# Feed-forward products and expert splits moved into the last cross-attention group's drain

## The chip, the cores and the metric

The kernel runs on one core of a Trainium2 chip. The metric is the time of one execution in device microseconds. Engines: PE (TensorE), ACT (ScalarE), DVE (VectorE), POOL (GpSimd), and SP, which issues most DMAs.

## The reference

A decoder layer in float32 with three residual stages, on x of 16 sequences of 128 tokens and width 256:

```python
x = x + attn(layernorm(x))            # 16 heads of 64, softmax without mask
x = x + xattn(layernorm(x), ctx)      # 16 heads of 16, masked, keys and values from ctx_1024
x = x + ffn(layernorm(x))

def ffn(x):                           # 8 experts, 256 -> 512 -> 256
    logits = x @ gate_w.T + gate_b    # rms-normalised, times rms_w, softmax(logits / 0.5)
    g = top_1(gates); norm_g = g / (g + 1e-6)
    h = gelu(einsum('nd,edh->neh', x, w1) + b1)
    y = einsum('neh,ehd->ned', h, w2) + b2
    return (y * norm_g[:, None, None]).sum(axis=1)
```

Each token goes through all eight experts.

## The kernel before, in words

Tokens are worked in 4 groups of 512 (4 tiles of 128). Three phases follow one another: ph 0 is self-attention, ph 1 cross-attention, ph 2 the feed-forward stage. Operands of products are split into a rounded high part and a low part (`hi` by ACT, `lo` by a DVE subtraction), and a product of two split operands is three matmuls (`three`, L490).

**Slots.** The attention phases are written as slots of a period of 16 (`run`, L311). In each slot every engine goes through its own hand-written order (`PE_ORDER`, `ACT_ORDER`, `DVE_ORDER`, `POOL_ORDER`), in which each step of a quad (scores, exponential, normalising, transposing, copying, product with V) has a lag in slots. At the end of a slot comes what the engine registered as `"slot"`. Behind the last period stands a drain of 20 slots (`DRAIN`), n = 0 to 19, with ph = 2: scores of the last quads in n up to 10, the last transposes in n = 13, the last product with V (quad 15) in n = 15, the second half of the output projection in n = 17 and 18, the residual in n = 18. The slot n = 4 begins near 525 us of the trace, n = 11 near 541.4, n = 15 ends at 551.03.

**Expert weights.** The 32 chunks m (8 experts x 4) of w1 and w2 come through a ring of four staging tiles `wst` (SP, L428). `expert_hi(m)` (ACT, L828) rounds a chunk into `arena`, `expert_lo(m)` (DVE, L880) writes the rest beside it. Four are split in slots 16 to 19 of the drain, behind a wait for the last product with V (`weights`, L830); the others one for each m in group 0 of the expert loop. Groups 1 to 3 find all of them in `arena`.

**The expert loop** (`experts`, L711 on PE, L851 on ACT, L1135 on DVE). PE runs `up(m)` (6 matmuls of 128x512, L490, into bank `H[m % 4]`) and `down(m - 2)` (12 of 128x256, L490, into Y), the gate's logits (L705) behind `up(1)`, and near the end the transposes of the next group's tokens (L651). ACT runs gelu(m) (L856) from `H` into `probs[m % 4]`, then hi(m) (L860) from there into `PT[m % 2]`; DVE runs lo(m) (L880). The waits that matter: `up(m)` for gelu(m-4), since it writes the same bank; hi(m) for `down(m-2)`, since it writes the same half of `PT`; `down(m)` for lo(m). On ACT the order is written out:

```python
for m in range(MCH):
    act.wait_ge(f1_ps, nth(MSTEP, 2, g, m))
    act.wait_ge(h_lo, nth(MSTEP_F4, 2, g, m - 4))
    act.activation(probs[:, m % 4, :], H[m % 4][:, :], ACT.Gelu, ...).then_inc(act_done, 1)
    act.wait_ge(act_done, nth(MSTEP_F4, 2, g, m))
    act.wait_ge(f2_ps, nth(MSTEP_F2, 2, g, m - 2))
    act.activation(PT[:, m % 2, 0, :], probs[:, m % 4, :], ACT.Copy).then_inc(h_hi, 1)
    if isinstance(g, int) and g == 0 and m + LEAD < MCH:
        expert_hi(m + LEAD)
```

`nth(count, ph, g, i)` is the semaphore value at which step i of group g is done; `_F4` and `_F2` add the 4 or 2 credits that POOL gives at the start.

Of the kernel before, what the change touches and what calls it, by code (L numbers as in the profile page):

```python
# [17 lines left out]
GROUPS = 4  # L18
TILES = 4
GT = TILES * P  # L20
QUADS = 16
# [23 lines left out]
def nth(count, ph, g, i):  # L45

    return count.credit + GROUPS * sum(count.per[:ph]) + g * count.per[ph] + i + 1
# [36 lines left out]
def build(nc, x, ctxT, mask, pieces, gateT, biases, rows, out):  # L84
    with ExitStack() as ctx:
# [78 lines left out]

        A0, A1, S0, S1, T, O, Y0, Y1 = (bank(n) for n in ("A0", "A1", "S0", "S1", "T", "O", "Y0", "Y1"))
        S, Y = (S0, S1), (Y0, Y1)
        H = (S0, S1, A0, A1)


        x_in = [sem("x_in0"), sem("x_in")]  # L170
# [94 lines left out]
        def steps(name, ph, g, v, lag=0):  # L265


            v -= lag
            if name == "quad":
                q = v - SCORES[ph]  # L270
                return [(q,)] if 0 <= q < QUADS else []
            if name in ("qk", "v"):
                if ph == 0:
                    j = v - XT_AT - 1
                    return [(j, BOTH)] if 0 <= j < 16 else []
                jobs = (QK1 if name == "qk" else V1)[g > 0]
                return [jobs[v]] if v in jobs else []
            if name in ("qk_out", "v_out", "qk_last", "v_last"):

                own = name.endswith("last")  # L280
                done = [j for j, halves in steps(name.split("_")[0], ph, g, v if own else v - 1)
                        if 1 in halves]
                return [(j,) for j in done if own == (ph == 0 and j == 15)]
            if name == "proj":
                q = v - SCORES[ph]
                if ph == 0:
                    return [(q // 2, (2 * (q % 2), 2 * (q % 2) + 1))] if 0 <= q < QUADS else []
                return {8: [(0, (0, 1))], 9: [(0, (2, 3))], 16: [(1, (0, 1))],
                        17: [(1, (2, 3))]}.get(q, [])
            if name in ("residual", "bias"):  # L290
                at = QUADS - 1 if ph == 0 else RESIDUAL1[g == GROUPS - 1]
                if name == "residual":
                    return [()] if v - SCORES[ph] == at else []
                part = v - SCORES[ph] - at - ((2, 0)[g == GROUPS - 1] if ph == 1 else 1)
                return [(part,)] if 0 <= part < 2 else []
            ahead = ph == 2 or ph == 1 and g > 0
            if name in ("stats", "norm"):
                tiles = (STATS1 if name == "stats" else NORM1)[ahead]
                return [(tiles[v],)] if v in tiles else []
            if name == "aggr":  # L300
                return [()] if v == AGGR1[ahead] else []
            if name in ("xt0", "xt1"):
                k = int(name[2])
                return [()] if v == (XT1[g > 0][k] if ph == 1 else XT_AT + k) else []
            if name in ("xt0_out", "xt1_out"):
                return steps(name[:3], ph, g, v - (ph == 1 and g > 0))
            if name == "ctx":
                return [(g + 1, v - 11)] if ph == 1 and g + 1 < GROUPS and 11 <= v < 15 else []
            raise ValueError(name)
# [13 lines left out]
        def attentions(eng, order, does):  # L323

            run(order, does, 0, 0, ())
            with eng.Fori(1, GROUPS) as g:
                run(order, does, 0, g, ((0, g - 1),))
            run(order, does, 1, 0, ((0, GROUPS - 1),), later=((1, 1),))
            for g in range(1, GROUPS):
                run(order, does, 1, g, ((1, g - 1), (1, g - 2))[:g],  # L330
                    later=((1, g + 1) if g + 1 < GROUPS else (2, 0),))
            run(order, does, 2, 0, ((1, GROUPS - 1), (1, GROUPS - 2)), DRAIN)

        DRAIN = 20
        TURN = 8
        LEAD = 4

        def v2(g, lo, job):

# [146 lines left out]
        def _(pe):  # L486
# [179 lines left out]
            for i in range(2):  # L666
                mm = pe.matmul(Y0[:, 0:D], ones[:, :], b2half[:, i, :], start=i == 0, stop=i == 1)
            mm.then_inc(b2_ps, 1)
            attentions(pe, PE_ORDER, {
                "scores": scores, "transpose": transpose_probs, "pv": probs_v, "proj": project_out,  # L670
                "qk": project_qk, "v": project_v,
                "xt0": lambda ph, g: transpose_group(ph, g, 0),
                "xt1": lambda ph, g: transpose_group(ph, g, 1)})

            def up(g, m):

                pe.wait_ge(act_done, nth(MSTEP_F4, 2, g, m - 4))
# [22 lines left out]
            def logits(g):  # L700
# [7 lines left out]
                                       start=i == 0, stop=i == 3)  # L708
                mm.then_inc(lg_ps, 1)

            def experts(g):  # L711
                last = isinstance(g, int) and g == GROUPS - 1
                for m in range(MCH + 2):
                    if m == MCH - 1 and not last:

                        transpose_tokens(2, g + 1, (T, O), ((lg_v, g * LGV + 1), None))
                    if m < MCH:
                        up(g, m)
                    if m == 1:
                        logits(g)  # L720
                    if m >= 2:
                        down(g, m - 2)

            with pe.Fori(0, GROUPS - 1) as g:
                experts(g)
            experts(GROUPS - 1)

# [2 lines left out]
        def _(act):  # L730
# [97 lines left out]
                act.activation(arena[:, at:at + PIECE], wst[:, m % 4, :], ACT.Copy).then_inc(e_hi, 1)  # L828

            def weights(ph, g, n):  # L830
                if ph == 2 and DRAIN - LEAD <= n < DRAIN:
                    if n == DRAIN - LEAD:

                        act.wait_ge(pv_ps, nth(SLOT_F2, 1, GROUPS - 1, QUADS - 1))
                    expert_hi(n - DRAIN + LEAD)
                if ph == 0 and isinstance(g, int):
                    for i in weight_slots(n):
                        weight_hi(i)
                    if n == 3:
                        act.wait_ge(b2_ps, 1)  # L840
                        act.activation(b2sum[:, :], Y0[:, 0:D], ACT.Copy).then_inc(b2_sum, 1)
                    if n == 15:
                        act.activation(gate[:, :, 0, :], gst[:, :].rearrange("p (k e) -> p k e", k=KD),
                                       ACT.Copy).then_inc(w_hi, 1)
# [33 lines left out]
        def _(dve):  # L878
            def sub_lo(out_, src, hi, sem_):
                dve.tensor_tensor(out_, src, hi.bitcast(F32), ALU.subtract).then_inc(sem_, 1)  # L880
# [142 lines left out]
            def xt_low(ph, g, k):  # L1023
                tokens_lo(ph, g, (A1, A0), (k,))

            def expert_lo(m):
                at = m * 2 * PIECE
                dve.wait_ge(e_hi, m + 1)
                sub_lo(arena[:, at + PIECE:at + 2 * PIECE], wst[:, m % 4, :], arena[:, at:at + PIECE],
                       e_split)  # L1030

            def weights(ph, g, n):
                if ph == 2 and DRAIN - LEAD <= n < DRAIN:
                    expert_lo(n - DRAIN + LEAD)
                if ph == 0 and isinstance(g, int):

                    late = weight_slots(n) if n < 8 else weight_slots(n - 1) if n > 8 else ()
                    for i in late + (weight_slots(n) if n == PERIOD - 1 else ()):
                        weight_lo(i)
                    if g == 0 and n == 12:  # L1040
                        constants()
                    if n == 15:
                        dve.wait_ge(w_hi, N1 + N2 + 1)
                        sub_lo(gate[:, :, 1, :], gst[:, :].rearrange("p (k e) -> p k e", k=KD),
                               gate[:, :, 0, :], w_split)
# [89 lines left out]
            def experts(g):  # L1135
                last = isinstance(g, int) and g == GROUPS - 1
                for m in range(MCH):
                    dve.wait_ge(h_hi, nth(MSTEP, 2, g, m))
                    sub_lo(PT[:, m % 2, 1, :], probs[:, m % 4, :], PT[:, m % 2, 0, :], h_lo)
                    if isinstance(g, int) and g == 0 and m + LEAD < MCH:  # L1140
                        expert_lo(m + LEAD)
                    if 4 <= m <= 11:
                        gating(g, m - 4)
                    if 14 <= m <= 18:
                        gating(g, m - 6)
                    if not last:
                        if 20 <= m < 24:
                            if m == 20:
                                dve.wait_ge(x_ready, nth(GRP, 1, g + 1, 0))
                                dve.sem_inc(dve_gate, 1)  # L1150
                            ln_stats(2, g + 1, m - 20)
                        if m == 24:
                            ln_finish(2, g + 1)
                        if m == 28:
                            ln_apply(2, g + 1, range(TILES))
                if not last:
                    tokens_lo(2, g + 1, (T, O))
                finish(g)
# [184 lines left out]
```

## Time and profile before

| | |
|---|---|
| median of 3 runs | 937.83 us (937.02 to 937.84) |
| profiled execution | 937.62 us |
| its span, first to last instruction | 935.8 us |
| mean granted TensorE clock | 0.986 |
| PE busy | 866.5 us (93%) |
| ACT busy | 630.3 us (67%) |
| DVE busy | 569.1 us (61%) |
| POOL busy | 291.6 us (31%) |
| clock row of the page, tenths, 40 slices of 23.4 us | 9999999999999999799999999999999999999999 |

The busy shares are means over stages with different limits. What a stage is bound by is read from its own stretch of the trace, and what an idle engine waited for stands in brackets behind the instruction that ended the idle time. A matmul's end is modelled, so that two groups of matmuls that follow each other overlap a little. The granted clock is a share of full speed: 1.00 is 2.4 GHz, 0.50 is 1.2 GHz.

### The profile page before, as it was taken

What the parts mean: (1) busy time and instruction counts of PE and PEld (TensorE: products, weight loads), DVE (VectorE), ACT (ScalarE), POOL (GpSimd) and SP (SyncE); (2) the same over time, 40 slices, a digit from 0 to 9 for tenths busy, and PEclk for the clock granted to TensorE, in tenths of its full rate; (3) what the DMA queues carried; (4) which work ended last, traced back from release to release, by engine and by line L of the source; (5) the groups of instructions that cost most, each with busy time, mean ns of one, the idle gap of its engine ahead of it and who ended that gap; (6) DMA issues with size and microseconds to landing.
All of it is one profiled execution on the core that took longest, in us unless ns stands there. A gap on an engine that the chain in (4) does not pass through costs nothing.

```text
span 935.8 us, 18382 instructions
## 1 busy us (share of the span) xinstructions
PE 866.5 (93%) x6274; PEld 782.3 (84%) x6274; DVE 569.1 (61%) x1172; ACT 630.3 (67%) x1764; POOL 291.6 (31%) x342
## 2 busy tenths in 40 slices
PE   4899999999999987899999879999999999999997
PEld 3788888889888876788888769999999999999996
DVE  4798888788878875677878755454223422342223
ACT  3897788788778864798989856765454445444543
POOL 2254454445445566655746540000000000000000
PEclk9999999999999999799999999999999999999999
DMA  6300000000000005665446113320000000000000
GB/s 207 122 31 18 1 1 1 0 0 0 0 0 0 1 1 137 144 160 113 142 86 171 45 35 102 95 87 6 17 0 0 8 15 0 0 14 9 1 1 22
DMA packets 21770, 41.98 MB, mean 45 GB/s; under 512 B 3144, under 2 KB 3152, under 8 KB 21712
## 3 DMA queue, kind: packets, MB, share of 16 engines
q1 hardware_dynamic: 21120, 40.91, 16.0%
q8 instruction: 32, 0.52, 0.3%
q10 hardware_dynamic: 592, 0.34, 0.2%
q14 instruction: 26, 0.21, 0.1%
HBM read 30.75 MB, written 10.49 MB: 44 GB/s over the span
## 4 chain that ended last, share of the span: by engine, by line
PE 64%; DVE 15%; ACT 13%; issue 5%; DMA 2%; POOL 1%; SPq 1%; DVEq 0%; ACTq 0%; POOLq 0%
PE Y L490 23%; PE A L490 20%; PE S L490 12%; ACT probs L803 7%; PE T L585 3%; DVE PT L880 3%; DVE nm L971 2%; DVE arena L940 2%; DVE oraw L990 2%; PE O L490 2%; PE O L602 1%; DVE arena L880 1%; ACT opart L817 1%; ACT PT L811 1%; DVE st L884 1%
## 5 line engine op out<-in xcount | busy, mean ns | idle before, releaser
L880 DVE TENSOR_TENSOR PT<-probs,PT 128x512 fp32r<-128x512 f32 x128 | 89.7, 701 | 230.9 <-ACT PT L860 230.9
L490 PE MATMUL A<-XT,arena 128*128 128x512 f32 x816 | 217.9, 401 | 6.3 <-DVE arena L940 5.3
L803 ACT ACTIVATE probs<-S,nm 128x128 f32<-128x128 f32 x512 | 181.5, 371 | 45.9 <-DVE nm L971 44.2
L490 PEld LDWEIGHTS Y<-arena,PT 128*128 128x128 f32 x1536 | 200.3, 191 | 11.0 <-DVE PT L880 1.1
L490 PE MATMUL Y<-arena,PT 128*128 128x256 f32 x1536 | 204.0, 283 | 0.3
L1194 POOL TENSOR_TENSOR probs<-probs,rinv 128x512 f32<-128x512 f32 x128 | 133.4, 1042 | 208.4 <-DVE rinv L976 208.3
L490 PEld LDWEIGHTS A<-XT,arena 128*128 128x128 f32 x816 | 144.7, 190 | 36.7 <-DVE arena L940 12.3
L860 ACT ACTIVATE PT<-probs 128x512 fp32r<-128x512 f32 x128 | 80.8, 631 | 90.7 <-PE Y L490 90.2
L803 ACT ACTIVATION_READ_ACCUMULATOR probs<-S,nm 128x1 f32 x512 | 107.4, 210 | 0.0
L880 DVE TENSOR_TENSOR PT<-T,PT 128x512 fp32r<-128x512 f32 x128 | 87.5, 684 | 25.0 <-ACT PT L811 22.8
L971 DVE TENSOR_REDUCE nm<-S 128x4 f32<-128x512 f32 x128 | 87.8, 686 | 18.0 <-PE S L490 10.5
L490 PE MATMUL S<-XT,arena 128*128 128x512 f32 x384 | 98.7, 394 | 0.0
L811 ACT ACTIVATE PT<-T 128x512 fp32r<-128x512 f32 x128 | 76.9, 601 | 23.7 <-PE T L585 21.1
L585 PE MATMUL T<-ident,probs 128*128 128x128 f32 x512 | 80.8, 281 | 5.3 <-DVE PT L880 3.4
L490 PEld LDWEIGHTS S<-XT,arena 128*128 128x128 f32 x384 | 68.7, 190 | 11.5
L490 PE MATMUL Y<-arena 128*128 128x256 f32 x480 | 72.0, 287 | 3.6 <-POOL arena L1216 3.6
L856 ACT ACTIVATE probs<-S,bias 128x512 f32<-128x512 f32 x64 | 44.0, 688 | 42.5 <-PE S L490 42.4
L490 PE MATMUL O<-PT,arena 128*32 128x128 f32 x768 | 60.2, 228 | 12.8 <-ACT oraw L822 7.3
L856 ACT ACTIVATE probs<-A,bias 128x512 f32<-128x512 f32 x64 | 44.0, 687 | 41.6 <-PE A L490 41.6
L990 DVE SCALAR_TENSOR_TENSOR oraw<-O,bias,opart 64x256 f32<-64x256 f32 x128 | 61.0, 477 | 16.5 <-ACT opart L817 14.9
L585 PEld LDWEIGHTS T<-ident,probs 128*128 128x128 f32 x512 | 57.3, 143 | 12.6 <-issue 6.7
L490 PEld LDWEIGHTS Y<-arena 128*128 128x128 f32 x480 | 64.3, 194 | 4.1 <-POOL arena L1216 3.9
(106 smaller groups left out, 1300.9 us busy)
## 6 DMA issues: line engine op xcount, KB each, us to landing
wst<-in_pieces SPq DMA_DIRECT2D x52, 256.0 KB, 2.7
stage<-arena SPq DMA_DIRECT2D x32, 256.0 KB, 2.3
arena<-stage SPq DMA_DIRECT2D x48, 128.0 KB, 4.1
arena<-stage SPq DMA_DIRECT2D x24, 256.0 KB, 3.9
xs<-in_x SPq DMA_DIRECT2D x4, 512.0 KB, 5.8
craw<-in_ctxT SPq DMA_DIRECT2D x4, 512.0 KB, 4.6
out<-craw SPq DMA_DIRECT2D x4, 512.0 KB, 2.6
rowc<-in_rows ACTq DMA_DIRECT2D x1, 264.0 KB, 5.5
```

What stands on the lines that cost most here:

```text
L490: mm = pe.matmul(acc, lhs[a], rhs[b], start=first and i == 0, stop=last and i == 2, skip_group_check=shared)
L585: mm = pe.transpose(T[:, u * P:(u + 1) * P], probs[:, n % 4, u * P:(u + 1) * P], ident[:, :])
L602: pe.matmul(O[:, u * P:(u + 1) * P], v4.rearrange("p s c -> p (s c)"), PT[:, n % 2, 0, u * P:(u + 1) * P], start=True, stop=False, skip_gr ...
L803: last = act.activation(probs[:, n % 4, u * P:(u + 1) * P], S[n % 2][:, u * P:(u + 1) * P], ACT.Exp, bias=nm[:, n % 4, u:u + 1], accum_out ...
L811: act.activation(PT[:, n % 2, 0, :], T[:, :], ACT.Copy).then_inc(pt_hi, 1)
L856: act.activation(probs[:, m % 4, :], H[m % 4][:, :], ACT.Gelu, bias=bias[:, B1 + m:B1 + m + 1]).then_inc(act_done, 1)
L860: act.activation(PT[:, m % 2, 0, :], probs[:, m % 4, :], ACT.Copy).then_inc(h_hi, 1)
L880: dve.tensor_tensor(out_, src, hi.bitcast(F32), ALU.subtract).then_inc(sem_, 1)
L940: last = dve.scalar_tensor_tensor(K[rows_, c % 2, 1, :, h, :], bank[rows_, :].rearrange("p (b c) -> p b c", b=TILES), bias[rows_, BK1 + c: ...
L971: dve.tensor_reduce(nm[:, n % 4, :], s3, axis=AX.X, op=ALU.max, negate=True).then_inc(maxed, 1)
L990: last = dve.scalar_tensor_tensor(oraw[h * DH1:(h + 1) * DH1, n % 2, 0:256].rearrange("p (b c) -> p b c", b=2), o4[:, :, h, :], bias[0:DH1 ...
L1194: pool.tensor_tensor(p3, p3, rinv[:, n % 4, :].unsqueeze(2).to_broadcast([P, 4, P]), ALU.mult).then_inc(normed, 1)
```

## The change

Splits of experts 0 to 5 are made in slots 4, 5, 6, 7, 12 and 13 of the drain instead of 0 to 3 in slots 16 to 19; `LEAD` becomes 6, so that the loop splits expert m + 6 in step m. PE computes `up(0)` to `up(3)` at the end of slots 11 to 14 and the logits and `up(4)` at the end of slot 16, ahead of the second half of the output projection; the banks `H` are ordered so that the first two are the ones that are free then. DVE makes lo(0) and lo(1) in slot 17, ahead of the residual. The token transposes of the feed-forward stage are issued one slot earlier on PE, their evacuation stays in its slot. In group 0 PE's loop starts at m = 5 and `down` lags `up` by 6 instead of 2; the transposes for group 1 stand at m = 34 of 38 instead of 31 of 34. DVE applies the layer norm of the next group at m = 26 instead of 28. Groups 1 to 3 are otherwise as before, and ACT's loop is not touched but for `LEAD`.

```diff
-        H = (S0, S1, A0, A1)
+        H = (A0, A1, S0, S1)
...
+            ahead = ph == 2 or ph == 1 and g > 0
...
-                return [()] if v == (XT1[g > 0][k] if ph == 1 else XT_AT + k) else []
+                return [()] if v == (XT_AT + k if ph == 0 else XT1[ahead][k]) else []
             if name in ("xt0_out", "xt1_out"):
-                return steps(name[:3], ph, g, v - (ph == 1 and g > 0))
+                return steps(name[:3], ph, g, v - ahead)
...
-        LEAD = 4
+        FIRST_EXPERTS = (4, 5, 6, 7, 12, 13)
+        LEAD = len(FIRST_EXPERTS)
+        UP_AHEAD = {11: (0,), 12: (1,), 13: (2,), 14: (3,), 16: (4,)}
+        LOW_AHEAD = (0, 1)
...
+            def experts_ahead(ph, g, n):
+                if ph == 2:
+                    if n == 16:
+                        pe.wait_ge(pt_lo, nth(SLOT_F1, 1, GROUPS - 1, QUADS - 1))
+                        logits(0)
+                    for m in UP_AHEAD.get(n, ()):
+                        if m in (2, 3):
+                            pe.wait_ge(exped, nth(SLOT_F2, 1, GROUPS - 1, QUADS - 4 + m))
+                        up(0, m)
+
+            attentions(pe, PE_ORDER, {
+                "slot": experts_ahead,
...
             def experts(g):
+                first = isinstance(g, int) and g == 0
                 last = isinstance(g, int) and g == GROUPS - 1
-                for m in range(MCH + 2):
-                    if m == MCH - 1 and not last:
+                lag = 6 if first else 2
+                for m in range(5 if first else 0, MCH + lag):
+                    if m == (MCH + lag - 4 if first else MCH - 1) and not last:
 
                         transpose_tokens(2, g + 1, (T, O), ((lg_v, g * LGV + 1), None))
                     if m < MCH:
                         up(g, m)
-                    if m == 1:
+                    if m == 1 and not first:
                         logits(g)
-                    if m >= 2:
-                        down(g, m - 2)
-
-            with pe.Fori(0, GROUPS - 1) as g:
+                    if m >= lag:
+                        down(g, m - lag)
+
+            experts(0)
+            with pe.Fori(1, GROUPS - 1) as g:
                 experts(g)
             experts(GROUPS - 1)
...
             def weights(ph, g, n):
-                if ph == 2 and DRAIN - LEAD <= n < DRAIN:
-                    if n == DRAIN - LEAD:
-
-                        act.wait_ge(pv_ps, nth(SLOT_F2, 1, GROUPS - 1, QUADS - 1))
-                    expert_hi(n - DRAIN + LEAD)
+                if ph == 2 and n in FIRST_EXPERTS:
+                    m = FIRST_EXPERTS.index(n)
+                    if m == 0:
+
+                        act.wait_ge(pv_ps, nth(SLOT_F2, 1, GROUPS - 2, QUADS - 1))
+                    if m == 4:
+
+                        act.wait_ge(scores_ps, nth(SLOT, 1, GROUPS - 1, QUADS - 1))
+                    expert_hi(m)
...
             def weights(ph, g, n):
-                if ph == 2 and DRAIN - LEAD <= n < DRAIN:
-                    expert_lo(n - DRAIN + LEAD)
+                if ph == 2 and n in FIRST_EXPERTS:
+                    expert_lo(FIRST_EXPERTS.index(n))
+                if ph == 2 and n == 17:
+                    for m in LOW_AHEAD:
+                        hidden_lo(0, m)
...
-                        if m == 28:
+                        if m == 26:
                             ln_apply(2, g + 1, range(TILES))
```

`hidden_lo(g, m)` is the pair of lines that was written out in DVE's loop before: the wait for hi(m) and the subtraction lo(m).

## Rows read from the trace of the kernel before

**Rows 1.** Busy time by stretches: us, PE, PEld, DVE, ACT, POOL, clock, DMA share, GB/s
```profile
525.50:535.60 10.10, 8.26 (x85) 6.94 (x83) 8.89 (x19) 9.62 (x41) 4.78 (x6) 1.00 0.00 1
...
541.46:551.03 9.57, 6.21 (x75) 5.04 (x73) 3.78 (x7) 4.47 (x13) 2.90 (x3) 1.00 0.01 2
551.03:554.28 3.25, 0.00 (x0) 0.00 (x0) 1.87 (x2) 3.19 (x6) 2.23 (x2) 1.00 0.01 1
554.28:557.50 3.22, 3.21 (x14) 3.12 (x15) 0.74 (x2) 0.96 (x1) 0.00 (x0) 0.50 0.59 162
...
557.02:650.56 93.54, 93.47 (x601) 84.99 (x601) 49.20 (x93) 60.28 (x97) 5.29 (x4) 1.00 0.25 74
650.56:930.00 279.44, 278.80 (x1794) 253.26 (x1792) 88.29 (x187) 136.65 (x205) 5.04 (x5) 1.00 0.02 6
```

**Rows 2.** Timeline (start us, us, what, idle before): the first products of group 1
```profile
650.56 2.91 PE L490 MATMUL S<-XT,arena 128*128 128x512 f32 x12
```

**Rows 3.** Timeline: a step of the expert loop in group 0
```profile
567.51 1.55 PE L490 MATMUL S<-XT,arena 128*128 128x512 f32 x6
...
568.90 1.59 PE L490 MATMUL Y<-arena,PT 128*128 128x256 f32 x12
...
569.10 0.69 ACT L856 ACTIVATE probs<-S,bias 128x512 f32<-128x512 f32 x1 [0.17 <-PE S L490]
...
570.33 1.55 PE L490 MATMUL S<-XT,arena 128*128 128x512 f32 x6
570.59 0.63 ACT L860 ACTIVATE PT<-probs 128x512 fp32r<-128x512 f32 x1 [0.80 <-PE Y L490]
571.13 0.62 ACT L828 ACTIVATE arena<-wst 128x512 fp32r<-128x512 f32 x1
```

**Rows 4.** Waits, 563 to 650: total us, times, longest
```profile
ACT PT L860 <- PE Y L490: 22.0, 28, 0.8
```

**Rows 5.** Timeline: the drain and the projection behind it
```profile
543.21 0.63 PE L585 MATMUL T<-ident,probs 128*128 128x128 f32 x4 [0.79 <-DVE PT L880]
...
543.76 0.68 ACT L822 ACTIVATE oraw<-O,bias 32x512 f32<-32x512 f32 x1
...
544.46 0.60 ACT L811 ACTIVATE PT<-T 128x512 fp32r<-128x512 f32 x1
...
544.58 0.88 PE L490 MATMUL O<-PT,arena 128*32 128x128 f32 x12 [0.75 <-ACT oraw L822]
545.09 0.69 DVE L880 TENSOR_TENSOR PT<-T,PT 128x512 fp32r<-128x512 f32 x1 [1.15 <-ACT PT L811]
...
554.29 2.93 PE L490 MATMUL Y<-arena 128*128 128x256 f32 x12 [3.27 <-POOL arena L1216]
...
557.26 1.29 DVE L1008 TENSOR_TENSOR xs<-Y,xs 128x512 f32<-128x512 f32 x2 [2.48 <-PE Y L490]
...
560.06 1.85 PE L705 MATMUL T<-gate,XT 128*128 128x16 f32 x16
```

**Rows 6.** Timeline of ACT: the gate's exponential at m = 12
```profile
594.32 1.28 ACT L866 ACT_TABLE_LOAD   x1
...
597.16 0.69 ACT L856 ACTIVATE probs<-S,bias 128x512 f32<-128x512 f32 x1
```

**Rows 7.** Timeline of PE: the idle time ahead of three groups of matmuls
```profile
21.31 2.54 PE L490 MATMUL A<-XT,arena 128*128 128x512 f32 x6 [2.26 <-DVE arena L940]
...
348.86 0.33 PE L602 MATMUL O<-PT,arena 128*128 128x128 f32 x1 [2.29 <-DVE PT L880]
...
517.07 0.88 PE L490 MATMUL O<-PT,arena 128*32 128x128 f32 x12 [1.26 <-DVE arena L880]
```

**Rows 8.** Busy time by stretches: behind two of these gaps, and from 373.50
```profile
21.90:25.00 3.10, 3.10 (x11) 2.50 (x9) 1.49 (x4) 1.11 (x3) 0.00 (x0) 0.50 0.58 184
...
348.86:352.00 3.14, 3.14 (x16) 2.85 (x17) 1.13 (x3) 2.52 (x10) 1.37 (x2) 0.60 0.01 3
...
373.50:387.00 13.50, 9.75 (x41) 8.10 (x42) 9.27 (x24) 8.53 (x42) 11.40 (x11) 0.50 0.86 179
```

More of the change, by code:

```diff
@@ L295, in steps @@
                 return [(part,)] if 0 <= part < 2 else []
-            ahead = ph == 2 or ph == 1 and g > 0
             if name in ("stats", "norm"):
@@ L668, in _ @@
             mm.then_inc(b2_ps, 1)
[L669 to L673, printed above, removed]
             def up(g, m):
@@ L709, in logits @@
                 mm.then_inc(lg_ps, 1)
+            def experts_ahead(ph, g, n):
[9 more added lines that the diff above has]
+                "slot": experts_ahead,
+                "scores": scores, "transpose": transpose_probs, "pv": probs_v, "proj": project_out,
+                "qk": project_qk, "v": project_v,
+                "xt0": lambda ph, g: transpose_group(ph, g, 0),
+                "xt1": lambda ph, g: transpose_group(ph, g, 1)})
             def experts(g):
+                first = isinstance(g, int) and g == 0
                 last = isinstance(g, int) and g == GROUPS - 1
-                for m in range(MCH + 2):
-                    if m == MCH - 1 and not last:
+                lag = 6 if first else 2
+                for m in range(5 if first else 0, MCH + lag):
+                    if m == (MCH + lag - 4 if first else MCH - 1) and not last:
                         transpose_tokens(2, g + 1, (T, O), ((lg_v, g * LGV + 1), None))
@@ L1024, in xt_low, with hidden_lo @@
                 tokens_lo(ph, g, (A1, A0), (k,))
+            def hidden_lo(g, m):
+                dve.wait_ge(h_hi, nth(MSTEP, 2, g, m))
+                sub_lo(PT[:, m % 2, 1, :], probs[:, m % 4, :], PT[:, m % 2, 0, :], h_lo)
             def expert_lo(m):
@@ L1137, in experts @@
                 for m in range(MCH):
-                    dve.wait_ge(h_hi, nth(MSTEP, 2, g, m))
-                    sub_lo(PT[:, m % 2, 1, :], probs[:, m % 4, :], PT[:, m % 2, 0, :], h_lo)
+                    if not (isinstance(g, int) and g == 0 and m in LOW_AHEAD):
+                        hidden_lo(g, m)
                     if isinstance(g, int) and g == 0 and m + LEAD < MCH:
```

## The prediction

> **What bounds the kernel now.** I read the busy shares stretch by stretch first. From the first up product of the feed-forward stage (557.02) to the end, TensorE is busy without a gap: 93.47 of 93.54 us in group 0, 278.80 of 279.44 in groups 1 to 3 [rows 1]. Group 0 runs from 557.02 to 650.56, where the first up product of group 1 starts [rows 1, 2]. Ahead of it lies the hole that the change aims at. In the drain of the last cross-attention group (541.46 to 551.03) TensorE has 6.21 us of work in 9.57; then it has none for 3.25 us while ACT and POOL turn the last output into weights for the output projection; then it runs 3.22 us at half clock (0.50) [rows 1]. The third reading is one step of the expert loop in the order of time [rows 3], and the waits of that loop [rows 4]: ScalarE's rounding copy into PT waits for the down product (PE Y) 28 times, 22.0 us in total. It costs nothing now. With it comes the chain that the change alters.
>
> **The order in the code.** ACT runs, for each chunk m, gelu(m), then hi(m) (the copy into PT[m%2]), in group 0 also the rounding of a later expert, then gelu(m+1). hi(m) waits until down(m-2) has read PT[m%2]. up(m) waits for gelu(m-4), because it writes into the same bank H[m%4]. Now PE runs up(m), down(m-2), so the ring down(m-2), hi(m), gelu(m+1), up(m+5) comes back to PE five steps after it left: slack. In group 0 of the changed kernel PE runs up(m), down(m-6). The ring becomes down(m-2), hi(m), gelu(m+1), up(m+5), **down(m-1)**: it advances by a single chunk, with all of its parts in series. PE runs up(6), down(0), and up(7) has to wait for gelu(3), which stands on ACT behind hi(2), which waits for down(0). This repeats for up(7) to up(31): 25 waits.
>
> **Part 1: expert splits in slots 4 to 7.** They add four ACT roundings and four DVE subtractions to a stretch where ACT is busy 9.62 of 10.10 us and DVE 8.89 [rows 1]. One rounding is 0.62 [rows 3]: 4 x 0.62 = 2.5, less the 0.48 that ACT has free = +2.0 us. Bounds: 0 (the slots are late for PE alone) and +2.5. DVE's four are 4 x 0.69 = 2.8 [rows 5] against 1.2 free, so +1.6 at most, beside ACT's and not on top; I take 2.0. The roundings queue ahead of the next slot's copies and exponentials on ACT, and the transposes wait for these. The transposes of the tokens come one slot earlier on PE and their copies stay: nothing. The loads of experts 4 to 7 are released earlier on SP, in a stretch without other transfers (DMA share 0.00 in [rows 1]): nothing. Splits 4 and 5 in slots 12 and 13 fall where ACT has 4.47 of 9.57 busy: nothing. What they free at the end (the old ones were done under POOL's split) is also nothing.
>
> **Part 2: up(0) to up(4) and the logits in the drain.** One up takes 568.90 - 567.51 = 1.39 us, one down 570.33 - 568.90 = 1.43 [rows 3], the logits 1.85 [rows 5]. A quad of the drain has 12 short products (0.88) and 4 transposes (0.63) [rows 5], about 1.25 where one group overlaps the next; its ring of transpose, ACT copy (0.60) and DVE subtraction (0.69) [rows 5] takes some 2.1 with the semaphores. With an up behind each transpose a slot takes 1.25 + 1.39 = 2.65, PE bound. Walked from the transpose at 543.21 (its 4 take 0.4 before the next can start): pv(12) 545.0, pv(13) 547.7, pv(14) 550.4, pv(15), whose slot before has no transpose, 552.6, its end 553.55, against 551.03: +2.5. Bounds: 0 (the ups fit into the idle time of 3.36 us) and 4 x 1.39 = +5.6 (nothing fits). Then the logits run to 555.3; ACT does the last output (0.68 [rows 5]), a table load for gelu (1.28 [rows 6]) and gelu(0) (0.69 [rows 3]), so up(4) starts about 556.4; the projection is next, at 557.8 and at full clock since no long gap is left; up(5) 559.3, up(6) 560.7, down(0) 562.1 (the residual add, 1.29 [rows 5], is done by 560.8), its end 563.7. With part 1: 565.7.
> Before, down(0) started at about 563.3 with ups 0 to 2 done; now it starts at 564.1 with 0 to 6 done. **The front gains** 4 x 1.39 - 0.8 = 4.8 us.
> Edits at nothing: lo(0) and lo(1) now stand ahead of the residual on DVE and wait for hi(1), which ACT has done at about 558.7, so they end about when the projection does (559.3); down(0), which waits for the residual, is covered by up(5) and up(6), 2.8 us. Without that cover it would cost up to 1.4 us. The new order of H only names free banks; the layer norm at m = 26 runs on a DVE that waits most of its time in the loop.
>
> **Part 3: the serial ring.** Behind the end of a down (568.90 + 1.59 = 570.49) come 0.10 until hi starts (570.59), 0.54 to the expert rounding (571.13) and 0.62 for it [rows 3], 0.69 for gelu, of which some 0.1 overlaps the rounding, and 0.14 until PE starts (as from 543.76 + 0.68 to 544.58 in the drain [rows 5]): about 2.0 us. The cycle is 1.45 (up, after a standstill) + 1.59 (down to its end) + 2.0 = 5.05 against 2.82. up(7) starts at 565.7 + 2.0 = 567.7; up(31) 24 cycles later: 24 x 5.05 = 121.2. Once, at m = 12, ACT loads two tables for the exponential of the gate: 597.16 - 594.32 = 2.84 [rows 6]. Before, the slack swallowed this; now it is in the ring: +2.9. Without the last rounding -0.5. up(31) starts at 691.3.
> The ScalarE: Activation LUTs page of the Trainium skill (What ACT_TABLE_LOAD costs) adds a drain of 1.38 us to each load; by it the two would cost 2.8 us more. The rows show the loads back to back at 1.28 and no drain [rows 6], so the sum leaves it out.
> Behind up(31) come down(25) to down(31) without an up between them. down(m) needs hi(m) (0.63) and lo(m) (0.69) after down(m-2), and with one down between, that is nearly hidden: from up(31) to the first up of group 1 I get 13.0 us, the token transposes included: 704.3. Before: 650.56 [rows 2]. **Sum at full clock: +53.8.** The profiled execution took 937.62 us (span 935.8), which lies 0.2 below the median of 937.83; from there 991.5.
>
> **Part 4: the clock.** In that loop TensorE stands still for 2.0 us in each 5.05. Every single gap of that order in the trace was followed by half clock: 2.26 us at 21.31 (0.50 in 21.90 to 25.00), 2.29 at 348.86 (mean 0.60 in the 3.14 us behind it), the 3.25 before 554.28; the 1.26 at 517.07 was not, by the profile page's clock row in the table [rows 1, 7, 8]. It came back while PE worked without a gap, 3.10 us from 21.90 and 3.21 from 554.28 [rows 1, 8]; at half clock the pair up and down is itself some 5.5 us of dense work. So I expect it to **fall and come back in turns**. A half-clock pair costs 2.93 - 1.59 = 1.3 for the down-like product of 12x256 [rows 3, 5] and at most 1.39 for the up (2.54 against 1.55 where part ran at full clock) [rows 3, 7]: about 2.55. Bounds: no pair (0) to all 25 (+64). I take 10 of 25, since the gap is a little shorter than those that lowered the clock and each fall lasts about one pair: +25.5. **991.5 + 25.5 = 1017.**
> The TensorE: Matmul & The Clock Gate page of the Trainium skill (Why this matters for your kernels) warns of idle gaps between bursts only when they are longer than this loop's. By that rule the clock stays full and the first rival below results; the rows of 2.26 and 2.29 speak against it, as these too are shorter than the page's.
>
> **Rivals.**
> 1. The clock stays full: 991.5. For it: the gap of 2.0 is shorter than any single one that lowered it, and between gaps lie 3 us of dense work. Against: it recurs 25 times.
> 2. The clock stays at half for nearly all of the loop: 991.5 + 24 x 2.55 = 1053. For it: from 373.50 to 387.00 it stayed at 0.50 with PE busy 9.75 of 13.50 us [rows 8]. Against: a half-clock pair gives 5.5 us of unbroken work, more than the 3.10 that raised it at 25.
> 3. Faster: the ring doesn't close, since ACT has gelu(m+1) done before down(m-2) ends. Then only the front's gain counts. Price: up(7) at 565.5, 24 x 2.82 to up(31), 13.0 to group 1: 646.2 against 650.56: 933.3. It decides at up(7). Against it: the 28 waits of hi for PE Y [rows 4], and ACT's order of gelu and hi is not touched by the diff.
> 4. The ups in the drain cost what they bring, and the ring stays open: 937.6, within 0.2%, which is about what a measurement of this kernel can tell from no change.
>
> **How the numbers follow.** Forecast (turns) 70%, rival 1 14%, rival 2 8%, a stall from elsewhere in group 0 that ends slower 3%, rival 3 4%, rival 4 1%. Slower 0.95, same 0.01, faster 0.04. Range: low end is rival 1 less the 2.0 of part 1 and 1.5 of reading error in the walk, 988; the high end takes 19 of 25 pairs at half clock, 1040. That leaves out rivals 2, 3 and 4 and little else.
>
> **What would show it.** In the profile after: ACT's copy into PT in group 0 starts 0.1 us behind each PE Y, and now PE's A and S products wait for ACT's gelu, 25 times, about 2.0 us each; PE is busy some 60% in group 0; the clock row shows digits below 9 in the slices from 570 to 700; group 1 begins near 730; groups 1 to 3 keep their 2.82 a step; the last pv ends near 555.5, and the projection starts without the 3.3 us gap. Wrong would be: PE waiting less than 1 us before an up (rival 3), or a wait for another engine in its place.

## The result, and the profile after

The changed kernel takes 1017.99 us (median of 4, 1016.85 to 1020.16) against 937.84 us (937.02 to 938.42): ratio 1.0858, 95% interval 1.0844 to 1.0871. The forecast was 1017. The profiled execution took 1017.41 us with a span of 1015.6, 79.8 us above that of before. The page:

```profile
PE 899.2 (89%) x6274; PEld 806.3 (79%) x6274; DVE 566.0 (56%) x1172; ACT 626.3 (62%) x1764; POOL 290.7 (29%) x342
...
PEclk9999999999999989999999877777999999999999
```

Between 558 and 711 us (the 23rd to the 28th slice) the clock row falls to 8 and 7, which it did nowhere in group 0 before. Now the loop of group 0, the lines of PE and ACT in the timeline (start, us, what, idle before). It is to be laid beside [rows 3], where up, down, up followed each other at 1.39 and 1.43 us:

```profile
562.40 1.63 PE L493 MATMUL S<-XT,arena 128*128 128x512 f32 x6 [0.69 <-DVE arena L901]
563.86 1.60 PE L493 MATMUL Y<-arena,PT 128*128 128x256 f32 x12
565.55 0.63 ACT L881 ACTIVATE PT<-probs 128x512 fp32r<-128x512 f32 x1 [4.84 <-PE Y L493]
566.09 0.61 ACT L845 ACTIVATE arena<-wst 128x512 fp32r<-128x512 f32 x1
...
566.61 0.67 ACT L877 ACTIVATE probs<-S,bias 128x512 f32<-128x512 f32 x1
...
567.33 1.65 PE L493 MATMUL S<-XT,arena 128*128 128x512 f32 x6 [1.87 <-ACT probs L877]
568.82 1.59 PE L493 MATMUL Y<-arena,PT 128*128 128x256 f32 x12
```

Down the column of starts stands the ring: down(0) at 563.86 ends at 565.46; hi(2) at 565.55; the rounding; gelu(3) at 566.61; up(7) at 567.33, after 1.87 us in which PE waited for gelu. Then the next down, and the same again. PE's waits over the whole execution, ended by gelu (L877), and the stretches (us, PE, PEld, DVE, ACT, POOL, clock, DMA share, GB/s):

```profile
PE A L493 <- ACT probs L877: 26.5, 13, 4.8
PE S L493 <- ACT probs L877: 23.8, 13, 1.9
```
```profile
542.56:554.48 11.92, 11.13 (x101) 9.50 (x99) 4.98 (x9) 5.50 (x15) 2.93 (x3) 1.00 0.16 45
567.33:717.03 149.70, 102.31 (x432) 87.22 (x432) 33.73 (x71) 43.75 (x74) 2.02 (x2) 0.77 0.12 35
717.03:730.39 13.36, 12.92 (x98) 12.26 (x99) 6.06 (x12) 6.44 (x11) 0.00 (x0) 1.00 0.00 1
```

Of these 26 waits 25 are those of up(7) to up(31); the other is up(4) in the drain. In the 149.70 us from up(7) to up(31) PE is busy 68%, at a mean clock of 0.77. Group 1 begins at 730.39 instead of 650.56 [rows 2]: +79.83, the whole difference of the spans. The clock inside the loop, four pairs of up and down of the same timeline:

```profile
591.45 1.66 PE L493 MATMUL S<-XT,arena 128*128 128x512 f32 x6 [1.87 <-ACT probs L877]
592.94 1.59 PE L493 MATMUL Y<-arena,PT 128*128 128x256 f32 x12
596.41 2.53 PE L493 MATMUL A<-XT,arena 128*128 128x512 f32 x6 [1.88 <-ACT probs L877]
598.74 2.30 PE L493 MATMUL Y<-arena,PT 128*128 128x256 f32 x12
602.90 2.24 PE L493 MATMUL A<-XT,arena 128*128 128x512 f32 x6 [1.87 <-ACT probs L877]
604.94 2.57 PE L493 MATMUL Y<-arena,PT 128*128 128x256 f32 x12
609.39 1.94 PE L493 MATMUL S<-XT,arena 128*128 128x512 f32 x6 [1.87 <-ACT probs L877]
611.12 2.76 PE L493 MATMUL Y<-arena,PT 128*128 128x256 f32 x12
615.76 1.65 PE L493 MATMUL S<-XT,arena 128*128 128x512 f32 x6 [1.87 <-ACT probs L877]
```

The waits are the same 1.87 us each time; what changes is the length of the products. Of these four pairs one is at full clock (4.96 us from start to start), the other three take 6.49, 6.49 and 6.37. In the whole loop it is 5 of 24.

### The profile page after: what moved, and what is told of

It is laid out like the page before. It is cut to its first block, busy times and chain, and to the rows that moved or that the text cites. A ratio compares the mean times of both kernels' runs of the same rounds, so it can differ in the third digit from the quotient of the medians.

```text
span 1015.6 us, 18344 instructions
## 1 busy us (share of the span) xinstructions
PE 899.2 (89%) x6274; PEld 806.3 (79%) x6274; DVE 566.0 (56%) x1172; ACT 626.3 (62%) x1764; POOL 290.7 (29%) x342
## 4 chain that ended last, share of the span: by engine, by line
PE 62%; ACT 15%; DVE 14%; issue 6%; DMA 2%; SPq 1%; POOL 0%; ACTq 0%; DVEq 0%; POOLq 0%
PE Y L493 22%; PE A L493 19%; PE S L493 12%; ACT probs L820 6%; PE T L588 3%; DVE PT L901 2%; PE O L493 2%; DVE nm L992 2%; DVE arena L961 2%; DVE oraw L1011 2%; ACT arena L845 2%; ACT probs L877 2%; PE O L605 1%; DVE arena L901 1%; ACT opart L834 1%
## 5 line engine op out<-in xcount | busy, mean ns | idle before, releaser
L493 PE MATMUL A<-XT,arena 128*128 128x512 f32 x816 | 225.1, 412 | 32.5 <-ACT probs L877 26.5
L493 PEld LDWEIGHTS Y<-arena,PT 128*128 128x128 f32 x1536 | 218.8, 208 | 13.0 <-DVE PT L901 1.7
L493 PE MATMUL Y<-arena,PT 128*128 128x256 f32 x1536 | 221.1, 299 | 0.6 <-DVE PT L901 0.4
L493 PEld LDWEIGHTS A<-XT,arena 128*128 128x128 f32 x816 | 148.2, 194 | 66.3 <-ACT probs L877 29.1
L493 PE MATMUL S<-XT,arena 128*128 128x512 f32 x384 | 105.2, 411 | 24.5 <-ACT probs L877 23.8
L1217 POOL TENSOR_TENSOR rstd<-ve,mhalf 128x4 f32<-128x4 f32 x12 | 12.2, 1015 | 225.4 <-DVE ve L916 225.4
L493 PE MATMUL A<-arena,XT 128*128 128x256 f32 x384 | 62.6, 299 | 5.3 <-DVE arena L901 3.3
L877 ACT ACTIVATE probs<-S,bias 128x512 f32<-128x512 f32 x64 | 43.7, 682 | 36.2 <-PE S L493 36.2
```

The lines of the kernel that those rows point to most:

```text
L493: mm = pe.matmul(acc, lhs[a], rhs[b], start=first and i == 0, stop=last and i == 2, skip_group_check=shared)
```

## The experiments

Each is compared with the kernel before on the same chip; where an interval is given, it is of the ratio.

**The lag alone.** Theory: the ring down(m-2), hi, gelu, up(m+5), down(m-1) is the loss. Rival: the work put into the drain is.

```diff
-                lag = 6 if first else 2
+                lag = 5 if first else 2
```

> The changed kernel with one number altered: down lags up by 5 instead of 6 in group 0. Theory (serial ring): with 5 the ring down(m-2), hi(m), gelu(m+1), up(m+5) comes back to PE one pair later, so 2.82 us of PE work lie beside ACT's 1.9 us and the waits vanish but for the one at m = 12 (two table loads, 2.9 us, less 0.9 of slack). down(0) at about 561.8, 26 pairs of 2.82, a tail of 11.8, 2 for the table loads: group 1 begins near 647, so about 934 us, below the kernel before. Rival (the loss comes from doing ups, logits and splits in the drain, or from the deeper lead as such): the waits ahead of the ups stay, and the time stays above 1000 us. If only a part of the ring opened, between 950 and 1000 us.

Measured: 936.77 us against 937.32 (ratio 0.9993, 0.9983 to 1.0003), 81 us less than the changed kernel by one digit. The drain keeps all that the change put there. PE's waits in the loop, and the place at m = 12:

```profile
PE A L493 <- ACT probs L877: 2.0, 1, 2.0
```
```profile
594.53 1.59 PE L493 MATMUL Y<-arena,PT 128*128 128x256 f32 x12
598.15 2.34 PE L493 MATMUL A<-XT,arena 128*128 128x512 f32 x6 [2.03 <-ACT probs L877]
600.29 2.48 PE L493 MATMUL Y<-arena,PT 128*128 128x256 f32 x12
```

24 waits are gone; the one at the two table loads is left, with a stretch of half clock behind it that I had not counted (2.34 and 2.48 against 1.55 and 1.59: from 598.15 to the next up at 602.61 it takes 4.46 instead of 2.82, 1.6 us). The time is 2.8 us above the forecast, and 1.9 of that is a slip in its sum: 561.8 + 26 x 2.82 + 11.8 + 2 is 648.9, not 647. Group 1 begins at 650.50, in an execution that was already 1.7 us behind that of the changed kernel ahead of all that the edit touches: the first scores products of the steady stretch that ends at 541 to 543 us ("the first scores" from here on) started at 396.3 and not at 394.6. The rest is inside the scatter (935.28 to 938.42).

**The lag without the drain.** The kernel before with

```diff
-        LEAD = 4
+        LEAD = 6
...
-                for m in range(MCH + 2):
+                lag = 6 if isinstance(g, int) and g == 0 else 2
+                for m in range(MCH + lag):
```

and `down(g, m - lag)`; no up and no logits in the drain.

> The kernel before with the lag of 6 in group 0 alone: all ups stay in the loop, nothing is moved into the drain; the six splits needed ahead stand in slots 14 to 19. Theory (serial ring): up(0) at 557.0, seven ups, the logits and down(0) to 570.2, then 25 waits of 1.9 us and the same clock as in the changed kernel (24 cycles in about 150 us), tail 13.4: about 1022 us, that is before + 84, more than the changed kernel by what its front gains (4 to 5 us). Rival (the drain part is to blame): about 938 us.

Measured: 1024.72 us (one execution). The lag alone costs 87 us, and the rest of the change brings back some 7. About 1 of these comes from the layer norm at m = 26: with the old m = 28 the transposes for group 1 wait 1.03 us for it at 730.69. PE's waits from 541 to 731 read as those of the changed kernel, though nothing but two more splits was put into the drain:

```profile
PE S L490 <- ACT probs L858: 25.4, 12, 4.8
PE A L490 <- ACT probs L858: 24.1, 13, 2.2
```

**The clock alone.** Five matmuls more behind each down of the ring:

```diff
                         down(g, m - lag)
+                        if first and m < MCH - 1:
+                            for _ in range(5):
+                                pe.matmul(O[:, :], identr[:, :], XT[:, 0, 0, :], start=True, stop=True)
```

> The changed kernel with five more matmuls of 128x512 behind each down in the ring, into bank O that nothing reads at that time: 1.07 us of PE work inside the 1.87 us of idle time, with no new wait. It shows the price of the clock alone. Theory (half clock in turns costs 28 us of the 80): granted clock 1.00 throughout, cycle 4.96, about 990 us though PE does 26 us more work. Rival (the clock is a by-product, and the fillers delay the ups or the clock falls all the same): 1018 us or more.

Measured: 994.85 us (one execution): 23 us less with 27 us of matmuls more. The cycle is 4.95 to 5.0 us, but for the one at the table loads:

```profile
570.23 1.64 PE L493 MATMUL S<-XT,arena 128*128 128x512 f32 x6 [0.71 <-ACT probs L880]
571.71 1.59 PE L493 MATMUL Y<-arena,PT 128*128 128x256 f32 x12
573.14 1.31 PE L741 MATMUL O<-XT,identr 128*128 128x512 f32 x5
575.18 1.66 PE L493 MATMUL A<-XT,arena 128*128 128x512 f32 x6 [0.73 <-ACT probs L880]
...
622.88 2.93 PE L493 MATMUL A<-XT,arena 128*128 128x512 f32 x6 [3.69 <-ACT probs L880]
625.61 2.74 PE L493 MATMUL Y<-arena,PT 128*128 128x256 f32 x12
```

So the clock is a cost of its own and not a by-product. Of the 5 us above the 990 expected, 2.4 are the half clock behind the table loads (7.34 us from 622.88 to the next up, instead of 4.98) and 1.4 that behind the logits in the drain, which the last experiment takes up. The rest, 1.4 us, was there ahead of the drain: the first scores came at 396.0 instead of 394.6.

**A shorter ring.** `expert_hi(m + LEAD)` stands between gelu(m) and the wait for down(m-2) instead of behind hi(m); nothing else is changed.

> The changed kernel with ACT's rounding of the next expert moved ahead of the wait for down(m-2), out of the ring. Theory: the wait ahead of each up shrinks from 1.87 to 1.33 us (by the 0.54 from hi to the rounding), the cycle at full clock from 4.96 to 4.42: 24 x 0.54 = 13 us less from the ring, about 1005 us if the clock falls as often as before; if the gap of 1.33 no longer lowers it (1.26 did not, 2.26 did), about 977 us. Rival (ACT's order is not what the ups wait for): 1018 us.

Measured: 978.29 us (one execution), against 977 for the case that the clock stays up. The rounding of 0.6 us is out of the ring, and with a gap of 1.36 us in place of 1.87 the clock stays at full:

```profile
566.96 1.66 PE L493 MATMUL S<-XT,arena 128*128 128x512 f32 x6 [1.36 <-ACT probs L877]
568.46 1.59 PE L493 MATMUL Y<-arena,PT 128*128 128x256 f32 x12
571.40 1.66 PE L493 MATMUL A<-XT,arena 128*128 128x512 f32 x6 [1.36 <-ACT probs L877]
```
```profile
566.96:610.00 43.04, 30.83 (x180) 26.20 (x180) 13.31 (x29) 16.00 (x28) 1.02 (x1) 1.00 0.21 62
```

Half a microsecond of ACT's order is worth 40 us here: 24 x 0.52 from the ring (4.96 to 4.44), and nearly all of the half clock (one fall is left, at 614.0 behind the table loads).

**The splits alone.** The changed kernel with `UP_AHEAD` and `LOW_AHEAD` empty, the logits back in the loop and the lag of 2.

> The changed kernel's splits in slots 4 to 7, 12 and 13 alone: no ups, no logits and no lo in the drain, the lag of 2 in every group. Theory: it carries the price of part 1 without any gain, since the four late splits of the kernel before lay beside POOL's split. In the traces so far the last scores stand 2.2 us later after the first ones near 400 than before; so +2.2, about 939.5 us. Rival (the splits are free, or less work at the end of the drain gives something back): 937.3 or below.

Measured: 939.78 against 937.88 (ratio 1.0017, 1.0008 to 1.0026). From the first to the last scores it takes 146.8 us (395.73 to 542.52) against 144.4 before (395.83 to 540.27). ACT is full in slots 4 to 7, where before it had 0.48 us free [rows 1]:

```profile
525.50:535.60 10.10, 7.31 (x73) 6.11 (x71) 9.22 (x19) 9.94 (x42) 4.16 (x4) 1.00 0.19 57
```

**The lag of 4.** down(0) behind up(5), down(1) and down(2) behind up(6), then `down(m - 4)`:

> The changed kernel with down lagging by 4 in group 0 (down(0), down(1) and down(2) behind up(5) and up(6), then one for each up). Theory: with the lag of 5 the ring has 0.9 us of slack, too little for the 2.9 us of the table loads at m = 12, which left a wait of 2.0 us and 1.9 us of half clock behind it; with the lag of 4 the slack is 3.7 us, and both go: 3.9 us less than with the lag of 5, about 933 us. Rival (the rest of the front's gain went elsewhere): 936 to 937 us, as with 5.

Measured: 934.96 against 937.88 (ratio 0.9969, 0.9956 to 0.9981), 1.8 us less than with the lag of 5 where 3.9 were forecast. At m = 12 PE no longer waits; two table loads lie beside two pairs:

```profile
594.41 1.28 ACT L891 ACT_TABLE_LOAD   x1
...
595.80 1.55 PE L493 MATMUL A<-XT,arena 128*128 128x512 f32 x6
595.95 1.28 ACT L881 ACT_TABLE_LOAD   x1
597.19 1.59 PE L493 MATMUL Y<-arena,PT 128*128 128x256 f32 x12
```

From the first scores to group 1 the trace has 251.8 us (396.09 to 647.87) against 254.2 with the lag of 5 (396.31 to 650.50), so 2.4 less, although here the clock fell behind the logits and there it didn't (up(4) to up(5) takes 4.25 us against 2.91). With these 1.3 us the gain of the loop itself is 3.7, close to the 3.9 of the forecast; the time doesn't show it whole.

**The tables alone.** The lag of 5, with `ACT.Copy` in the place of `ACT.Exp` in ACT's loop.

> The kernel with the lag of 5 with the gate's exponential replaced by a copy in all groups, so that ACT loads no table at m = 12. It leaves out the exponential of the gate's softmax. Theory (the table loads are what is left in the ring): the 2.0 us of wait and the 1.9 us of half clock go, nothing else does: 936.8 - 3.9 = 933 us, the same as the kernel with the lag of 4. In groups 1 to 3 the loads lie in slack: nothing. Rival: 936.8 us.

Measured: 933.63 against 937.88 (ratio 0.9953, 0.9940 to 0.9967), 3.1 us below the lag of 5 with the loads, where 3.9 were forecast. ACT loads no table behind 558.21, PE waits for nothing at m = 12, and from the first scores to group 1 the trace has the 251.8 us of the lag of 4 (397.50 to 649.29), with the same fall of the clock behind the logits. So the loads were what was left in the ring of the kernel with the lag of 5.

**The splits four slots later**, `FIRST_EXPERTS = (8, 9, 10, 11, 12, 13)`, with the lag of 4:

> As the kernel with the lag of 4, and with the first four splits in slots 8 to 11 instead of 4 to 7. Theory: slots 4 to 7 are ACT's bound (9.62 of 10.10 us busy before), slots 8 to 10 are PE's and slot 11 leaves ACT some idle time, so 1 to 2 us of the 2.2 come back: 931.5 us. Rival: slots 8 to 10 have only 0.6 us free on ACT, so the price moves with the splits and the time stays within 0.5 us of the kernel with the lag of 4.

Measured: 933.58 (ratio 0.9957, 0.9943 to 0.9970), 1.4 below the kernel with the lag of 4; their intervals overlap, so that the times don't settle it. The forecast was 931.5. The scores take 145.5 us (395.62 to 541.10), so that 1.3 of the 2.3 us come back there. But by up(4) they are gone again: from the first scores to up(4) it is 162.5 us (to 558.11), against 162.65 with the splits in slots 4 to 7 (396.09 to 558.74). The subtraction for the split of slot 11 now stands on DVE ahead of the one into PT for which the next transposes wait:

```profile
546.40 0.69 DVE L905 TENSOR_TENSOR arena<-wst,arena 128x512 fp32r<-128x512 f32 x1 [2.06 <-ACT arena L849]
...
547.10 0.66 DVE L905 TENSOR_TENSOR PT<-T,PT 128x512 fp32r<-128x512 f32 x1
...
547.90 0.63 PE L588 MATMUL T<-ident,probs 128*128 128x128 f32 x4 [0.69 <-DVE PT L905]
```

So the trace speaks for the rival: most of the price moved with the splits. Group 1 begins 2.0 us earlier than in the execution profiled with the lag of 4 (645.86 against 647.87): 1.3 of it is the clock, which stayed up behind the logits here, and 0.5 was there at the first scores.

**The gap behind the logits.** With the change PE runs the logits behind the last product with V and waits 1.03 us for gelu(0). The same order gave two things: of the seven profiled executions that have it, three ran the next 3 us or so at half clock and four did not (I had counted six). First the execution of the changed kernel, then that with the fillers, PE's timeline:

```profile
554.32 1.90 PE L702 MATMUL T<-gate,XT 128*128 128x16 f32 x16
...
557.25 1.64 PE L493 MATMUL A<-XT,arena 128*128 128x512 f32 x6 [1.03 <-ACT probs L877]
...
558.73 1.60 PE L493 MATMUL Y<-arena 128*128 128x256 f32 x12
```
```profile
558.74 1.92 PE L493 MATMUL A<-XT,arena 128*128 128x512 f32 x6 [1.03 <-ACT probs L880]
560.46 2.77 PE L493 MATMUL Y<-arena 128*128 128x256 f32 x12
563.02 1.70 PE L493 MATMUL A<-XT,arena 128*128 128x512 f32 x6
```

Last experiment: as the kernel with the lag of 4 and the late splits, with `UP_AHEAD = {11: (0,), 12: (1,), 13: (2,), 16: (3, 4)}` and the logits between up(3) and up(4).

> As the kernel with the lag of 4 and late splits, with up(3) behind the last product with V, ahead of the logits, instead of a slot earlier. Behind the logits PE stands still for 1.03 us until gelu(0) is done, and of the six profiled executions with that order three ran the next 3 us at half clock (about 2.5 us longer) and three did not. Theory: up(3), 1.4 us, fills that gap, so it can't lower the clock; the last product with V comes 0.9 us earlier, since its slot then is bound by the ring of copies (2.1 us) and not by PE (2.65): together 0.5 us of idle time less and on average 1.2 us of half clock less, about 932 us. Rival (the work only moves, the gap opens in the slot before, and the clock falls as often): 933.6 us.

Measured: 931.05 us (930.21 to 931.90) against 937.48 (ratio 0.9929, 0.9915 to 0.9942). From up(3) to group 1 PE doesn't wait, and group 1 begins at 644.01:

```profile
553.14 1.60 PE L493 MATMUL S<-XT,arena 128*128 128x512 f32 x6
554.58 1.85 PE L702 MATMUL T<-gate,XT 128*128 128x16 f32 x16
556.28 1.61 PE L493 MATMUL A<-XT,arena 128*128 128x512 f32 x6
557.73 1.59 PE L493 MATMUL Y<-arena 128*128 128x256 f32 x12
```
```profile
557.00:645.00 88.00, 87.84 (x575) 80.03 (x575) 47.15 (x91) 54.52 (x93) 5.32 (x4) 1.00 0.23 67
```

From the first scores to up(4) it takes 161.3 us (395.00 to 556.28) against 162.5: 1.2 us less, so that the work doesn't merely move. This is all order, and no clock, since the execution profiled with up(3) in its old place had full clock behind the logits too. That up(3) keeps the clock up there isn't shown: one execution stayed at 1.00 with it, and four of seven did without it.

This is the fastest of all and beats both kernels: what the change was after, with a lag that leaves its ring open.

## Why the prediction was right

**The ring** (part 3) was the loss, as put: 25 waits, and a lag of 5 takes 24 of them away with nothing else changed, while a lag of 6 in the kernel before brings them all. The size of the cycle was 5.05 by the sum and 4.96 in the trace: the wait is 1.87, not 2.0, since gelu begins 0.52 us behind the start of the rounding and not behind its end.

**The front** (part 2) came within fractions: from pv(11) to the end of pv(15) 11.92 us against 9.57 [rows 1], +2.35 where I had +2.5; up(7) at 567.33 against 567.7. The second is closer than it should be, by luck: this execution had its first scores at 394.6 instead of 395.8, 1.2 us early, so that up(7) is 0.8 us late against the forecast. Missed on the way: up(6) waited 0.69 us for the split of expert 6, which stands on DVE behind lo(0), lo(1) and the residual. I had asked only who waits for the residual, not who waits for what is queued behind it. Part 1, +2.0 by the sum, is 2.3 in the changed kernel (146.7 us between the first and the last scores, 394.64 to 541.38, against 144.4 before) and 1.9 in time for the splits alone.

**The table loads** cost 4.84 - 1.87 = 2.97 us, once, against 2.9. They are the two loads of 1.28, the exponential of 0.23 between them and 0.18 between the instructions. The Trainium skill (ScalarE: Activation LUTs, What ACT_TABLE_LOAD costs) adds a drain of about 1.38 us to each load. This place shows no such drain: by it PE would have waited 2.8 us longer here.

**The clock** (part 4) was the term with the widest bounds. From up(7) to up(31) the trace has 149.70 us; 24 x 4.96 + 2.97 - 0.52 (the last wait is 1.35) = 121.5, so 28.2 are the clock's, where I had 25.5. The two misses, -2.1 in the ring and +2.7 in the clock, cancel by luck; the time of 1017 is closer than its terms. Inside the clock's term two more errors cancel. I had 10 pairs at 2.55 us each; in the trace 19 of the 24 cycles are longer, by 1.5 us on the mean, since the clock falls and rises within them and 5 alone are at full clock. So the mechanism, falls and returns in turns, was right, and its size was right by luck. The fillers confirm it from the other side: up(7) to up(31) takes 124.2 us instead of 149.7, 25.5 less, and with the 2.4 of the fall that remained it is 28. In this loop a repeated 1.87 us lowered the clock again and again, and a repeated 1.36 us did not. The Trainium skill (TensorE: Matmul & The Clock Gate, Why this matters for your kernels) asks to avoid only gaps between bursts that are longer than both. The loop with 1.87 us does not bear that out: it lost 28 us to the clock. Where the limit lies is open, and whether it is one of the gap or of the cycle, since the two changed together.

**The tail** took 13.36 us against 13.0. The layer norm at m = 26, which I put at nothing, saves about 1 us there (the kernel without it waits 1.03 us at 730.69). I did not see that a lag one smaller would have taken away nearly the whole loss; the walk of part 3 had all the numbers for it, 2.82 us of PE work against 1.9 of ACT's.

## What to carry to other kernels

Before one engine is let run ahead of another, write down the ring of buffers by which it comes back, and count by how many steps the ring advances in one turn: here H has 4 banks and PT 2, so that a lag of 6 is serial and a lag of 4 or 5 is open. A ring with little slack is closed again by a single long instruction in it (two table loads), so leave slack for the longest one. A small wait that repeats in a dense loop can cost twice, by itself and by the clock: here 1.87 us in each 4.96 did, and 1.36 in each 4.44 cost only itself.

## What the runs showed of the hardware

The granted clock depends on repeated gaps more finely than I had read from single ones [rows 7, 8]: 0.77 on the mean with 1.87 us in each 4.96, 1.00 with 1.36 in each 4.44.

Nor does a single gap of one length always do the same. The one ahead of the matmul near 349 us [rows 7] is in all eleven profiled executions, 2.28 to 2.30 us long. In nine of them the clock fell to 0.50 at its end or within 2 us of it, in two (the lag without the drain, the shorter ring) it did not. From the execution of the shorter ring, PE's line and the stretch behind it, at a clock of 1.00:

```profile
349.03 0.33 PE L605 MATMUL O<-PT,arena 128*128 128x128 f32 x1 [2.28 <-DVE PT L901]
```
```profile
349.03:352.00 2.97, 2.97 (x22) 2.71 (x23) 0.96 (x3) 2.34 (x10) 1.19 (x2) 1.00 0.01 3
```

And of seven profiled executions with 1.9 us of logits (16 columns each) and then 1.03 us without work, three ran about the next 3 us at 0.50 and four did not; with up(3) in the gap the one profiled execution stayed at 1.00. A gap of 1.26 us at 517.07 did nothing [rows 7], with other work ahead of it. Which of the two, the gap or the work ahead of it, makes the difference was not tried.
